# Third norm of a four-layer graph network: halves of two batches in place of the whole group

## What is computed

```python
def _layernorm(x, axis=-1, eps=1e-05):
    m = jnp.mean(x, axis=axis, keepdims=True)
    v = jnp.var(x, axis=axis, keepdims=True)
    return (x - m) / jnp.sqrt(v + eps)

x = _layernorm(x + _L0(x, ...))   # two gated neighbour sums, a gated loop, relu
x = _layernorm(x + _L1(x, ...))   # neighbour sum, 128->256->128 with two batch norms
x = _layernorm(x + _L2(x, ...))   # attention over the graph:
    # Wh = x @ W;  e = leaky(Wh @ a1 + (Wh @ a2)^T) masked by adj
    # attention = softmax(e);  result = attention @ Wh
x = _layernorm(x + _L3(x, ...))   # two graph convolutions, then four LSTM passes:
    # for p in 1..4: an LSTM of p steps over windows of p nodes, its last state
    # replaces the last node of each window
```

## Time and profile before

| | us |
|---|---|
| median of 3 runs | 687.6 (686.8 to 688.49) |
| the profiled execution's own time | 687.35 |
| its span in the trace | 685.5 |
| TensorE busy in the span | 643.4 (94%) |
| VectorE busy | 461.2 (67%) |
| ScalarE busy | 407.9 (60%) |
| GpSimd busy | 247.3 (36%) |
| longest line of the chain that ended last | L749, 22% |

### The profile page before, as it was taken

How to read it: one execution, slowest core, us unless ns; L and a number is a source line. 1 busy time by engine, 2 the same in 40 slices (tenths; PEclk the granted TensorE clock), 3 DMA queues, 4 the chain that set the end, 5 groups by cost and what they waited for, 6 DMA issues and landing times.

```text
span 685.5 us, 9202 instructions
## 1 busy us (share of the span) xinstructions
PE 643.4 (94%) x2818; PEld 445.7 (65%) x2818; DVE 461.2 (67%) x1338; ACT 407.9 (60%) x819; POOL 247.3 (36%) x250
## 2 busy tenths in 40 slices
PE   8899988996799999999999999999999999999993
PEld 6656646445685587578568757855875685576573
DVE  5968885678875657757865776687577665454444
ACT  3767765865835675475567547565754765456552
POOL 4797981005643033520433152143215303300301
PEclk9999999999999999999999999999999999999997
DMA  9223000000000000000000000000000000000000
GB/s 354 94 99 154 1 1 0 1 0 1 0 1 1 0 1 1 1 32 1 1 32 0 1 1 31 1 1 32 1 0 1 31 1 1 31 1 0 32 0 31
DMA packets 4225, 16.75 MB, mean 24 GB/s; under 512 B 464, under 2 KB 464, under 8 KB 4048
## 3 DMA queue, kind: packets, MB, share of 16 engines
q1 hardware_dynamic: 4176, 16.16, 6.1%
HBM read 11.97 MB, written 4.19 MB: 24 GB/s over the span
## 4 chain that ended last, share of the span: by engine, by line
PE 62%; DVE 10%; POOL 5%; ACT 4%; issue 2%; DVEq 0%; POOLq 0%; ACTq 0%
PE QQ L749 22%; PE QQ L761 13%; PE PA L732 4%; PE QQ L624 4%; PE PA L703 3%; POOL X L473 2%; POOL RSD L378 2%; PE PB L723 2%; DVE STL L1167 2%; PE PB L713 2%; PE PA L692 2%; PE PA L667 2%; PE PB L692 2%; PE PB L654 2%; ACT raw L1016 1%
## 5 line engine op out<-in xcount | busy, mean ns | idle before, releaser
L1009 ACT ACTIVATE raw<-QQ,BL 128x256 f32<-128x256 f32 (+2 forms) x312 | 168.8, 562 | 117.3 <-PE QQ L761 80.2
L749 PE MATMUL QQ<-HT,WT 128*128 128x256 f32 (+2 forms) x624 | 204.6, 472 | 3.9 <-DVE HT L1418 3.3
L378 POOL TENSOR_TENSOR RSD<-VAR,pw 128x8 f32<-128x8 f32 (+1 forms) x36 | 58.7, 1629 | 282.0 <-DVE VAR L1189 282.0
L749 PEld LDWEIGHTS QQ<-HT,WT 128*128 128x128 f32 x624 | 116.3, 190 | 65.7 <-issue 31.6
L761 PE MATMUL QQ<-HB,WT 128*128 128x256 f32 (+2 forms) x384 | 114.4, 441 | 2.0 <-DVE HB L1418 1.9
L1396 DVE SCALAR_TENSOR_TENSOR raw<-raw 128x512 f32<-128x512 f32 (+2 forms) x88 | 50.3, 571 | 66.0 <-ACT raw L1009 65.2
L761 PEld LDWEIGHTS QQ<-HB,WT 128*128 128x128 f32 x384 | 69.9, 190 | 35.5 <-issue 15.3
L1016 ACT ACTIVATE raw<-raw 128x512 f32<-128x512 f32 (+2 forms) x88 | 45.1, 513 | 42.1 <-DVE raw L1406 32.4
L492 POOL TENSOR_TENSOR HB<-HB 128x512 f32<-128x512 f32 x28 | 35.1, 1272 | 93.5 <-ACT HB L968 93.5
L1418 DVE SCALAR_TENSOR_TENSOR HB<-raw 128x256 f32<-128x256 f32 (+2 forms) x48 | 24.0, 499 | 29.3 <-ACT raw L1016 29.3
L1418 DVE SCALAR_TENSOR_TENSOR HT<-raw 128x512 f32<-128x512 f32 (+2 forms) x40 | 24.2, 604 | 23.2 <-ACT raw L1016 23.2
(11 more groups left out here) (180 smaller groups left out, 1067.8 us busy)
## 6 DMA issues: line engine op xcount, KB each, us to landing
raw<-in_xt SPq DMA_DIRECT2D x8, 512.0 KB, 6.1
four<-in_x SPq DMA_DIRECT2D x8, 512.0 KB, 4.6
out<-four SPq DMA_DIRECT2D x7, 512.0 KB, 2.6
WT<-in_lstm SPq DMA_DIRECT2D x1, 2048.0 KB, 8.1
later<-in_later SPq DMA_DIRECT2D x1, 662.0 KB, 8.4
AD<-in_adj SPq DMA_DIRECT2D x1, 512.0 KB, 4.7
out<-four SPq DMA_DIRECT2D x2, 256.0 KB, 2.1
early<-in_early SPq DMA_DIRECT2D x1, 274.0 KB, 3.1
```

What stands on the lines that cost most here:

```text
L378: pool.tensor_tensor(RSD[kk][:, ts], VAR[kk][:, ts], pw[:, ts], ALU.pow).then_inc(ln[k]["rstd"], some)
L749: mm = pe.matmul(steps_view(Q[q], k), WT[:, 0, (p - 1) * 4 + q, :], ht_view(par, k), start=True, stop=(s == 0))
L1009: act.activation(TG[q][:, 0:n], Q[q][:, 0:n], ACT.Tanh, scale=0.5 if q == G else 0.25, bias=BL[:, p - 1, q:q + 1]).then_inc(g_ok, 1)
```

## The change

The third norm of a slot's group is done as two halves. On VectorE the first half (batches 0 and 1, four tiles: statistics and the six small operations, `a_norm2(s, 0)`) stands ahead of the sum of batch 3, and so ahead of `cell(10)`; `a_stats2` and `a_small2` keep their places but treat the second half only. On POOL `rstd` and `scale2` run once for each half at the end of the slot, and `scale2` no longer opens the next slot. Its tiles, results and semaphores are the same, and TensorE and ScalarE have the same instructions as before.

```diff
             def slot(s, par, A, B, L, T):
-                if B:
-                    scale2(s - 1)
                 if A:
                     rstd(1, 0, s)
                 if T:
@@
                 if A:
                     weights(s, range(GB))
                     scaled(s + 2)
-                    rstd(2, 1, s)
+                    for h in range(2):
+                        rstd(2, 1, s, h)
+                        scale2(s, h)
@@
             rstd(2, 2, 1, 0)
             rstd(2, 2, 1, 1)
+            scale2(1)
             slots(slot)
@@
             def a_stats2(g):
                 dve.wait_ge(z2_ok, TILES * (g + 1))
-                norm_tiles(2, front(g).kk2, front(g).Z2, g)
+                norm_tiles(2, front(g).kk2, front(g).Z2, g, 1)
 
             def a_small2(g):
-                norm_small(2, front(g).kk2, g)
+                norm_small(2, front(g).kk2, g, 1)
@@
                 cell(9)
                 if A:
+                    a_norm2(s, 0)
                     a_sum2(s, (3,))
                     a_stats2(s)
                 cell(10)
```

## The result

| | before | after |
|---|---|---|
| median of the runs, us | 687.58 | 682.4 (681.56 to 683.17, 4 runs) |
| ratio to before | | 0.9924 [0.9906, 0.9942] |
| the profiled execution's own time, us | 687.35 | 681.96 |
| its span, us | 685.5 | 680.1 |

The changed kernel is 0.76% faster: 5.2 us by the medians, where 4.2 were forecast.

The account below looks back on a forecast made before the run. TensorE, busy 94%, waited most for POOL's scaled third-norm tiles (5.5 us in 13 waits). Five turns 3.0 plus last turn 1.2 make 4.2 off 687.35, 683.15; plus 0.25 for the median, 683.4 us, range 681.8 to 687.6.

Parts of the forecast that it names:

- Step 10's start: VectorE, end of step 9's state to step 10's first product: 3.20 us instead of 3.02, 0.18 later.
- The port: VectorE's step 10 beside POOL's scalings, through the port both share: stretched by twice 0.05, so 0.10 us.
- that rival: Shared port: each POOL scaling holds VectorE in full, 693.2 us; chance 0.14 for delay beyond 1.1.
- The second set of small operations: VectorE behind step 10, six small operations for the second half: 0.85 us instead of 1.07, 0.22 less.
- d: Delay on VectorE behind the second small operations, at step 0's first product, against before: 0.05 us.
- `x(2)`: TensorE in the turn: starts at 395.3 instead of 396.59, 1.3 us won there.
- The new wait of L647: TensorE (L646 before the change) waits for VectorE's apply of the second norm: about 0.5 us, five times.
- The restart: TensorE's short transposes behind the new stall take longer: 0.2 us, ends 0 and 0.27.
- The rest of the slot: Behind L646, where VectorE and ScalarE had waited for TensorE anyway: moves up as a whole.
- A turn: Each of five turns with part A gains 0.60 us; slots 60.25 us apart and not 60.85.
- the formula: Gain over all turns: 5 x (0.65 - d) + (1.25 - d) = 4.5 - 6d; 4.2 us at 0.05.
- The last turn: No part A behind it, so no L646: `x(2)` starts at 577.86 instead of 579.06, 1.2 us.

Follow-up runs that it names:

- e1: Changed kernel, but POOL takes both powers first and then scales all eight tiles: 685.82 us, 0.9975 of before.
- e5: Changed kernel, but POOL scales the first half twice, the first time into a scratch tile nobody reads: 682.78 us, 0.994 of before.
- e2: Changed kernel, but the second norm of a whole group raises its semaphores by one, not two: 680.64 us, 0.9899 of before.
- e6: Kernel before, but the third norm of a whole group raises its semaphores by one, not two: 686.43 us, 0.9985 of before.
- e4: Changed kernel with ten unread VectorE operations, about 0.85 us, behind the third norm's small operations: 686.7 us, 0.9986 of before.
- e9: Changed kernel, split kept on POOL, but all statistics and both sets of small operations on VectorE not ahead of step 10: 685.4 us, 0.9977 of before.
- The repeated kernel: The changed kernel timed again, nothing altered, beside later runs on the same chip: 681.34 us, 0.9917 of before.
- the ballast kernels: Kernel before and changed kernel, each with ten unread VectorE operations behind the third norm's small operations: 687.46 us (1.0001) and 686.7 us (0.9986).
- e7: Changed kernel, but the first half's four statistics stand between products and state of step 9: 679.34 us, 0.9887 of before.

## Why the prediction was right

Times are from the end of step 9's state.

- **Step 10's start** was forecast at 3.20 without the port, and came at 385.25 - 382.05 = 3.20. The idle 0.61 was used up as said.
- **The port** was sized at 0.10 and cost VectorE 0.05 (the state of step 10 takes 0.47, and 0.42 in e1, where POOL rests). e5 shows that it isn't more there with twice the scalings. The reading under the prediction was wrong, though: it took the 0.05 as speaking against a lock that blocks VectorE fully. The 0.05 is what such a lock leaves, since the state started with 0.19 of a scaling left; what failed in that rival is its price, a full 0.43 for each scaling. It was mostly POOL that gave way: its first half was ready at 384.91 + 2.36 - 382.05 = 5.22 and not 4.6, its second at 11.1 and not 10.3. L704 asked for them at 9.2 and 13.6, so it cost nothing here; in e1 it did.
- **The second set of small operations** was taken at 0.85 and took 388.29 - 387.47 = 0.82. It is shorter because it counts by one, which the prediction did not name (e2, e6).
- **d** was forecast +0.05 and is 6.15 - 6.20 = -0.05.
- **`x(2)`** was to win 1.3 us and won 12.21 - 10.91 = 1.30. It lost 0.10 of it at once: its six matmuls took 2.84 where they took 2.74.
- **The new wait of L647** was the right wait in the right place (e2, e4, e9), and mis-sized: 0.17 instead of about 0.5. The apply came 0.24 earlier relative to step 9 than forecast, 0.10 of it by d and 0.10 by a shorter power (1.97 against 2.07), and TensorE came 0.11 later, mostly by the longer `x(2)`.
- **The restart** was taken at 0.2, from 1.13 against half of 1.73, 0.27 more. These two are not of a kind. In the chain a group that follows TensorE's own work counts from the end of the group before, and one behind a wait from its own start, so the 1.13 holds some 0.17 that is no loss. By the starts, L703's four held `x(2)` up for 0.96 before (395.46 to 396.42) against 0.87 for half of the eight after, 0.10 more; L647's eight cost 0.06 (0.93 to the next group after, 0.87 before).
- **The rest of the slot** was to move up as a whole, and did not quite. L647 starts 19.08 behind step 9's state, before 19.95 (404.16), 0.87 earlier. But from L647 to the next step 9's state it is 41.06 (from 340.99) against 40.90 (from 343.31): 0.06 of that is L647's longer group, most of the rest is lost in steps of the LSTM some 14 us behind it.
- **A turn** was to give 0.60 and gave 0.72 (60.84 to 60.12). By the formula with the measured d it is 0.65 + 0.05 = 0.70. That this fits to 0.02 is in part luck: the formula leaves out the shorter power (0.10) and the loss in the rest of the slot (0.10), which cancel. The same formula gives 0.18 for e9 (measured 0.18) and -0.03 for e4 (measured -0.13, and -0.03 over the three slots without the gap).
- **The last turn** was to give 1.2. The timeline there, before and then after:

```profile
578.90 2.74 PE L749 MATMUL QQ<-HT,WT 128*128 128x512 f32 x6
```

```profile
572.52 0.79 DVE L1419 SCALAR_TENSOR_TENSOR HT<-raw 128x512 f32<-128x512 f32 x1 [0.76 <-ACT raw L1017]
...
573.36 2.84 PE L750 MATMUL QQ<-HT,WT 128*128 128x512 f32 x6
```

  Behind step 9's state (562.35; 566.69 before) `x(2)` starts at 11.01 and not 12.21, 1.20 earlier as forecast, and takes 2.84 against 2.74, so 1.10 is left. The number came out by another limit than the one named: TensorE's own path would have been there at 573.26, eight matmuls of 1.73 behind L704's start at 571.53. What came last was the state of step 1, which ends at 573.31 and took 0.79 where it took 0.71 before, beside a scaling of POOL.

The sum of the six is 5 x 0.72 + 1.10 = 4.7 us. The span is 5.4 us shorter; the remaining 0.7 lies ahead of the slots, where both kernels have the same code. There the last matmuls ahead of the slots started at 203.88 before and 203.15 after, and between 201.38 and 204.94 over the 13 profiled executions. That part is not the change's. The repeated kernel has 60.10 per slot.

What stays open: why one slot of e6 is longer, what the gap in the ballast kernels is, by which rule TensorE's first group behind a wait is longer, and why the LSTM steps behind a late L647 lose time.

## What to carry to other kernels

When a wait is removed, follow the chain that arrives next and write the gain as a function of its delay; ballast of known length in both kernels then shows whether that chain binds. A split pays by the half that starts early, so the producer has to hand it on before it begins the second. Fill the gaps inside a step before lengthening the path (e7), and count semaphores by one where a set of tiny dependent operations is on the chain (e2). A view that lists no wait does not show that none is left. And check a reading of two rows for whether both count from the same point: the chain and the timeline do not.

## What the runs showed of the hardware

- Six small dependent operations of VectorE take 1.07 us when each raises its semaphore by two and 0.86 when by one, on the same 16 and 8 columns (e2, e6). By two, the waits between them are instructions of their own.
- VectorE and POOL beside each other: four scalings of POOL took 1.73 us alone, 2.36 beside step 10 and 3.27 in the turn; a power of four columns 1.01 alone and 1.39 when it started while a product of VectorE with both operands in SBUF ran (388.38 against 388.20). VectorE lost 0.05 at step 10 and 0.18 in the last turn of e5. The Trainium skill, page "SBUF — State Buffer", section "Who interferes with whom", has an exclusive lock that blocks the other engine fully. The 1.40 us in the earlier trace rows agree with it, and so do the ends of the operations above, on both sides: POOL's long scalings end 0.16 to 0.33 behind VectorE's operation, VectorE's 0.27 or 0.53 and more behind POOL's scaling. Its price to VectorE was small here because a scaling is short (0.45) and VectorE came when little of it was left. Whether longer instructions of POOL at this place would hold VectorE for longer was not tried.
- A short wait of TensorE costs more than itself: counted from start to start, the group behind it was 0.06 longer for eight transposes (L647) and 0.10 for four matmuls (L703 before).
